# First cross attention: the second half of head 0's keys copied within SBUF

## The reference, cut to what matters

```
q = heads(layernorm(x));  k = v = heads(ctx_1024)        # 16 heads, d_k = 16
u = einsum('hbqd,hbkd->hbqk', q, k) * scale / sqrt(d_k)
logits = tanh(u) * exp(log_C);  logits[mask] = -inf
out = softmax(logits) @ v                                # per head
x = x + out.reshape(...) @ W_out.T
```

## Time and profile before

| | |
|---|---|
| median of three runs | 775.89 us |
| the profiled execution | 776.85 us, of it 775.1 us from the first to the last instruction |
| TensorE, matmuls | 619.4 us busy (80%) |
| ScalarE | 464.7 us (60%) |
| VectorE | 417.9 us (54%) |
| GpSimd | 71.7 us (9%) |
| DMA, whole kernel | 73.41 MB, mean 95 GB/s |

### The profile page before, as it was taken

The page is one execution under the profiler, slowest core; times in us unless marked ns, Lnnn a source line. Parts: engine busy times, 40 slices in busy tenths (PEclk is TensorE's granted clock), DMA queues, the critical chain, the costliest instruction groups (busy, mean ns, idle before and its releaser), DMA issues. The chain is left out here.

```text
span 775.1 us, 14282 instructions
## 1 busy us (share of the span) xinstructions
PE 619.4 (80%) x4872; PEld 381.6 (49%) x4872; DVE 417.9 (54%) x921; ACT 464.7 (60%) x558; POOL 71.7 (9%) x148
## 2 busy tenths in 40 slices
PE   2696768788878876497369999999998699845997
PEld 1353434444444343275235555555554567634886
DVE  6564541322322314765578898988982436345443
ACT  3896959999999964273036676776776047203010
POOL 3010201000100003000110101111110100000000
PEclk9998979999999985699568999999999599979799
DMA  5877754476443104000622222332220900000000
GB/s 132 217 215 221 247 174 114 129 206 185 121 119 112 48 22 148 0 1 1 222 65 63 86 80 78 86 79 81 85 63 1 336 30 2 1 0 1 1 0 14
DMA packets 52695, 73.41 MB, mean 95 GB/s; under 512 B 10866, under 2 KB 29618, under 8 KB 52658
## 3 DMA queue, kind: packets, MB, share of 16 engines
q1 hardware_dynamic: 51890, 72.19, 31.7%
q10 hardware_dynamic: 768, 0.73, 0.3%
HBM read 58.89 MB, written 12.85 MB: 93 GB/s over the span
## 5 line engine op out<-in xcount | busy, mean ns | idle before, releaser
L1550 DVE TENSOR_REDUCE sb_m_blk<-ps 128x1 f32<-128x512 f32 x256 | 159.6, 684 | 22.1 <-PE ps L1408 20.9
L1359 ACT ACTIVATE sb_probs<-ps 128x1024 f32<-128x1024 f32 x128 | 125.9, 1025 | 52.5 <-PE ps L1438 51.3
L644 ACT ACTIVATE sb_probs<-ps 128x1024 f32<-128x1024 f32 x128 | 124.0, 1017 | 24.9 <-PE ps L690 22.3
L648 ACT ACTIVATE sb_probs<-sb_probs,sb_neg_cap,sb_cap 128x4096 f32<-128x4096 f32 x32 | 121.6, 3801 | 1.1
L707 PE MATMUL ps<-sb_probs,sb_v_st 128*32 128x256 f32 x1024 | 77.0, 398 | 38.3 <-ACT sb_probs L648 38.3
L1408 PE MATMUL ps<-sb_k_st,sb_q_m 96*128 96x512 bf16 x256 | 91.1, 400 | 2.7 <-DVE sb_m_blk L1550 2.1
L690 PE MATMUL ps<-sb_q_st,sb_k_st 112*128 112x256 bf16 x512 | 76.8, 286 | 5.2 <-DMA sb_k_st<-k_parts_l 4.0
L1438 PE MATMUL ps<-sb_q_st,sb_k_st 115*128 115x256 bf16 x512 | 77.7, 275 | 1.4 <-ACT sb_probs L1359 1.4
L690 PEld LDWEIGHTS ps<-sb_q_st,sb_k_st 112*128 112x128 bf16 x512 | 46.4, 101 | 49.4 <-ACT sb_probs L644 23.9
L1454 PE MATMUL ps<-sb_probs,sb_v_st 128*32 128x256 f32 x1024 | 67.4, 384 | 0.2 <-ACT sb_probs L1359 0.2
L1438 PEld LDWEIGHTS ps<-sb_q_st,sb_k_st 115*128 115x128 bf16 x512 | 49.3, 98 | 19.2 <-issue 2.5
(11 more groups left out here) (254 smaller groups left out, 825.1 us busy)
## 6 DMA issues: line engine op xcount, KB each, us to landing
sb_k_st<-k_parts_l SPq DMA_DIRECT2D x223, 64.0 KB, 2.0
sb_k_st<-k_parts_l SPq DMA_DIRECT2D x93, 128.0 KB, 3.1
k_parts_l<-sb_v_proj SPq DMA_DIRECT2D x24, 256.0 KB
k_parts_l<-sb_early SPq DMA_DIRECT2D x48, 128.0 KB
sb_v_proj<-ctxT_blocks SPq DMA_DIRECT2D x8, 512.0 KB, 8.3
sb_early<-ctxT SPq DMA_DIRECT2D x8, 512.0 KB, 3.8
sb_v_rows<-ctx_by_pair SPq DMA_DIRECT2D x7, 512.0 KB, 4.3
sb_k_st<-k_parts_l SPq DMA_DIRECT2D x64, 32.0 KB, 1.7
```

The lines of the kernel that those rows point to most:

```text
L644: a.activation(probs[:, j % 2, 4 * g:4 * g + 4, :], scores_bank(g), ACT.Tanh).then_inc(s["tanh"], 1)
L648: a.activation(probs[:, j % 2], probs[:, j % 2], ACT.Exp, bias=k.neg_cap[:, 0:1], scale=k.cap[:, 0:1]).then_inc(s["exp"], 1)
L1359: sc.activation(probs[:, g], scores_bank(g), ACT.Exp).then_inc(s["exp"], 1)
L1550: v.tensor_reduce(k.m_blk[:, b, q, blk:blk + 1], k.ps[:, m_bank(m_turn_of(idx)), :], AX.X, ALU.max).then_inc(s["m_read"], 1)
```

## The change

Folds 2 and 3, the second half of head 0's keys, are copied within SBUF as folds 0 and 1 are, by 14 DMAs of 32 KB (2 x 7), all issued by SyncE. They go to slot 1 of `k_st` and count on the semaphore that the load of slot 1 had. `load_first(0, 1)` is gone. The copies stand behind the last copies of unit 0 and ahead of the stores of block 0's middle and low part. `load_block(1)` moves ahead of the wait for block 0's stores. The wait of TensorE for slot 1 is written for the new count.

```diff
     def first_slot(eng, fold, row, part):
-        eng.dma_start(k.k_st[row:row + DH, 0, fold * KSPLIT:(fold + 1) * KSPLIT],
-                      parts[2 * DH * fold:2 * DH * fold + DH, 0, part]).then_inc(first_in[fold], 16)
+        eng.dma_start(k.k_st[row:row + DH, fold // 2, fold % 2 * KSPLIT:(fold % 2 + 1) * KSPLIT],
+                      parts[2 * DH * fold:2 * DH * fold + DH, 0, part]).then_inc(first_in[fold] if fold < 2 else k_in[1], 16)
...
             for fold in range(2):
                 first_slot(sp, fold, MAXROW, 2)
+            for fold in range(2, 4):
+                first_hi(sp, fold)
+                first_mid(sp, fold)
+                first_slot(sp, fold, MAXROW, 2)
             for p in (1, 2):
                 store_part(k, sp, 0, p, parts)
+            load_block(k, sp, 1, blk)
             sp.wait_ge(k.sem("k0_stored0"), blocks_stored(0))
-            load_first(0, 1)
-            load_block(k, sp, 1, blk)
             for j in range(2, 4):
                 load_first(0, j)
...
                 elif g == 0:
-                    pe.wait_ge(k_in[j], 16 * K_LOADS * (it if j == 0 else it + 1))
+                    pe.wait_ge(k_in[j], 16 * K_LOADS * (it if j < 2 else it + 1) + (32 * FIRST_LOADS if j == 1 else 0))
```

## The result

The changed kernel takes 781.08 us (median of 6 runs, 780.14 to 782.68) against 776.43 us for the kernel before in the same comparison: a ratio of 1.0058, 95% interval 1.0033 to 1.0083. A second measurement, of twelve executions, gave 781.58 us, ratio 1.0062 (1.0039 to 1.0084). So it is slower by some 4.5 us. The direction held. The range (774.5 to 781.5) held by only 0.4 us, and the second median lies just above it. The size was put too low: +2.4 us, against the three executions of the kernel before as against the profiled one, which in fact went from 776.85 to 780.88 us.

The account below looks back on a forecast made before the run. SyncE's queue and DMA chain, through block 1's stores landing, was taken as the bound: 42.3 to 44.7, +2.4 us carried to the end, 776.85 to 779.25, median 0.96 below, forecast 778.3 us; range 774.5 to 781.5.

Parts of the forecast that it names:

- What bounds this stretch: First 107 us: SyncE's queue and the DMA engines set the time, by when block 1's stores have landed, 42.30.
- The copies' issue and unit 1's keys: SyncE from 14.34: 14 issues of 0.606 us last until 22.8; unit 1's keys at 24.6, 0.8 us later.
- The third rival: TensorE's start of unit 1: keys before 23.78, up to 0.8 us gained, 775.1 us; chance 0.10.
- The stores of block 0 and the reorder: SyncE: unit 2's keys 6.2 us later, slack covers most, block 1's stores out at 35.0; moving load_block(1) costs nothing.
- The backlog: DMA engines: 2.56 MB burst lasts until 39.3; block 1's stores queue behind it, landing 43.4 to 45.7, taken as 44.7.
- the missing hole at 34: DMA share at 34 us: the drop to 0.05 seen before would not come in the changed kernel.
- the full share until 39: DMA engines in the changed kernel's timeline: share full until 39 us.
- VectorE's late split of block 2: VectorE: split of block 2 ends at 43.3, the copy behind it 2.5 us late; priced at nothing.
- the stand: ScalarE's idle 7.17 us until 68.13 in the first cross attention; swallows what unit 1 gains or loses before 61 us.
- Absorption: SyncE's queue, 42.30 to 57.16: a later start finds emptier engines, 2.2 us come back, 776.1 us; chance 0.18.
- The second stand: ScalarE's idle 7.96 us until 107.06, after TensorE's wait for context; +2.4 us carried through to 109.5.
- The dearer rival: SyncE's issues at 829 ns, or a store behind both loads: 779.3 to 783 us, chance 0.14.

Follow-up runs that it names:

- the early split: Kernel before, with load_block(1) ahead of the wait for block 0's stores and split_block(1) ahead of turned_to_stack(0) on VectorE: 773.14 us, ratio 0.9968.

## Why the prediction was right in kind and short in size

**What bounds this stretch: right, and shown.** The chain over block 1's stores sets the time: 14 idle DMA issues in the kernel before give a loss of the same size, and the early split there gives a gain.

**The copies' issue and unit 1's keys: right.** Forecast until 22.8 and keys at 24.6; measured 23.3 and 24.69. The third rival (keys before 23.78) didn't come about. The trace after has 22 such issues by SyncE, 0.59 us in the median against 2.0 us to landing. The rule of the Trainium skill that the time to initiate is "usually small relative to the DMA itself" ("DMA: Bandwidth & Descriptors", section "Issuing engines are not separate DMA queues") isn't met by DMAs this small, where it is 0.59 of 2.0 us, and the measurement decides. The section names no size for which it holds.

**The stores of block 0 and the reorder: the failed step.** I wrote that "moving load_block(1) ahead costs the wait nothing". It costs the wait 1.2 us (6.67 us in place of 5.46), shown in two pairs, with and without it. That, the copies' extra 0.5, and slower issues (the 14 behind the wait took from 30.01 to 37.52, 7.5 us in place of 6.7; one issue of 1.10 us among them) made the queue 2.5 us later than forecast: 37.5 in place of 35.0. Since VectorE's split was over at 35.27, all of the extra lateness counted. As a sum it is the whole of what was missing: the chain moved by 4.85 us where I had 2.4. Two things in it are open. What made the issues slower isn't shown: the DMA share was 0.61 from 30.0 to 33.2 and 0.87 beside the slow issue, while before the same 14 issues went through in 6.7 us at a share of 1.01. And with the reorder undone in the changed kernel, block 1's stores landed no sooner (47.25), so its share of the 4.85 us isn't shown either.

**The backlog: right size, wrong picture.** From the issue of block 1's stores to landing it took 47.15 - 37.56 = 9.6 us, 1.2 more than the 8.4 of before; I had put in 1.3. But the engines weren't full from 24 until 39: the share was 0.61 from 24 to 34 and 0.64 over the whole stretch. Of the two signs that I gave for the engines, the missing hole at 34 came (0.63 in place of 0.05), the full share until 39 didn't. The same bytes came later and less dense, and block 2 landed at 43.7, not 39.4. That the term came out at the right size is luck, as far as the traces show.

**VectorE's late split of block 2, priced at nothing: held.** The copy behind it ran at 47.62 in place of 40.78, 6.8 us late where I had 2.5, and TensorE waited 0.6 us for a split behind it. ScalarE's waits at units 3 and 4 (2.30 and 1.42 us) were swallowed by the stand, as said, and SyncE didn't wait.

**Absorption: none up to the first stand, a little at the second.** The +4.85 at 47.15 became +5.2 at the context block's issue, +5.35 on TensorE (69.29) and +5.8 on ScalarE (73.96). The last half microsecond is TensorE's clock: granted 0.51 (1.2 of 2.4 GHz) from 63.9 to 67.5 before, after 7.31 us without work, and full from there; in the changed kernel, after 9.67 us, still 0.50 to 0.51 from 69.3 to 75.0, so that the eight `qk` matmuls of 1.04 us at 67.49 took 1.91 us at 72.86. One unit later ScalarE was 6.3 us late (78.62 against 72.28). The second stand, 6.64 us in place of 7.96, gave 1.3 of them back. So the queue's delay wasn't carried on unchanged, as I had written, but nearly so. The slow issues that I thought might give 2.2 us back (3.51 us for three) took 3.77 us. I had called the engines full there; the share was 0.80. Of the +5.0 at 112.08, 0.4 went within that unit (idle 0.33 in place of 0.73), +4.6 stayed to the last unit, and the profiled executions end with 4.0; where the last 0.6 us went, in later stages, isn't shown.

The dearer rival (chance 0.14) put 779.3 to 783, and the time is there, but by another term than its slow issues of 829 ns.

## What to carry to other kernels

Each of these small copies cost what stands behind it in its queue 0.6 us of issue, at 64 bytes a row as at 2 KB. Before taking a round trip out in favour of many small copies, count issues x 0.6 us against the wait removed, and look which later transfers stand in the same queue. A wait that is removed from one consumer may be still needed by the next one, as the wait for block 0's stores was here; then nothing is gained but the first consumer's time. Price what moves beside the change as well: the reorder to which I gave no price has a loss of 0.7 to 3.6 us by itself. And find the event that a queue's stretch hangs on (here: block 1 stored) and move its producers into idle time: that gained 0.4% where the change lost 0.6%.

## What the runs showed of the hardware that I had not expected

- Issue time of a copy within SBUF didn't fall with its size: 0.59 us in the median for 16 rows of 64 bytes and for 16 rows of 2 KB; a load of 32 rows of 4 KB from DRAM took 0.43.
- A load of 512 KB issued right behind two stores of 256 KB lengthened their landing: 6.5 to 6.8 us from first issue to release in the seven traces with it, 5.3 to 5.5 in the four without.
- GpSimd issued the 14 copies in 6.92 us, 0.49 each, less than SyncE. But beside them SyncE's own copies within SBUF took 4.9 us to landing in place of 2.4.
- SyncE's issues weren't slower for full DMA engines alone: 14 took 6.7 us at a share of 1.01 in the kernel before, and 7.5 us at 0.61 to 0.87 in the changed one.

```profile
8.25 6.92 POOL L446 DMA_DIRECT2D sb_k_st<-sb_v_proj  x14 [4.23 <-ACT sb_v_proj L632]
```
